# Experts' down projection of a four-layer kernel: weights stationary, output turned back by PE

## The chip, the cores and the metric

One core of one Trainium2 chip runs the whole program in one launch. The metric is the device time of that launch in microseconds (us). The engines are PE (matrix multiply; PEld is its loading of the stationary operand), DVE (vector), ACT (activation), POOL (GpSimd) and SP (which issues DMAs and raises semaphores).

## What is computed

The reference is a chain of four blocks on x of shape (4, 1024, 128), all in float32: `x = x + layernorm(block(layernorm(x)))`, with block = an attention of 16 heads, a latent attention followed by a mixture of experts, a second attention of 16 heads, and a low-rank feed-forward. The change lies in the mixture of experts:

```python
def _experts(x_flat, Wg, Wu, Wd):
    g = silu(einsum('nc,eci->nei', x_flat, Wg))
    u = einsum('nc,eci->nei', x_flat, Wu)
    return einsum('nei,eic->nec', g * u, Wd)
shared = mean(_experts(xf, sWg, sWu, sWd), axis=1)          # one shared expert
probs = softmax(xf @ Wgate + expert_bias)
topk_p, topk_i = top_k(probs, 2); topk_p /= sum(topk_p)
comb = sum(one_hot(topk_i, 8) * topk_p[..., None], axis=1)
routed = einsum('ne,nec->nc', comb, _experts(xf, Wg, Wu, Wd))
return shared + routed                                      # then residual, layernorm, residual
```

There are 8 routed experts and one shared one, of 64 inner columns each, and 128 channels. All of them are computed for every token; the gate weight of a token multiplies the inner columns before the down projection, so that one accumulation over all inner columns gives shared + routed.

## The kernel before, in words

The program is a sequence of phases, each closed by a barrier of all engines (`end_phase`, L109): projection and attention of the first block, the latent attention, `experts()` (L1681 to L1953), projection and attention of the third block (`prepare("a1")` and what follows), and the last block. Semaphores of a phase are made by `sem(name)` (L96), which has SP raise each new one to BASE = 1, one instruction for each (L101).

**Tiling of `experts()`.** The 4096 tokens lie as 32 tiles of 128 tokens on the partitions. The four batch entries b are the bodies of the phase; each has two chunks u of CH = 512 tokens, and a chunk has CT = 4 tiles t. The 9 experts are paired: GP = 5 groups j, four with 128 inner columns (two experts) and one with 64 (the shared one). `run_sequences` (L1721) runs `front(0)`, then a hardware loop over bodies 0 to 2, `body(b, b + 1)`, and then `body(3, None)` apart. Each engine has its own order, written out by hand, and the engines meet only at semaphores.

**PSUM.** It has eight banks of 512 float32 columns. Bank 0 holds turned x or a group's spread gate weights, bank 1 the logits and turned gates, banks 2 and 3 gate projections, 4 and 5 up projections, banks 6 and 7 (`6 + u`) the down projection of chunk u.

**A body on PE** (L1826): for each of the ten (u, j), the gate and up matmuls (L1834, L1836; weights stationary, 512 tokens moving) and the spreading of gate weights (L1841). Then, if a body follows, `logits(b + 1)`: four transposes for each chunk (L446) and eight matmuls with 8 moving columns (L1805). Then the down projection (L1849 to L1855): for each chunk, each of its 4 tiles and each of the 5 groups, a matmul with 128 tokens of `hT` as stationary operand and the 128 channels of `wd` moving. Last `turn_gates(b + 1)` (L1815), which needs the gates from DVE (s_g).

**A body on DVE** (L1922): the ten products silu x up (L1930) and product x gate weight (L1935). Then `front(b + 1)`, the gates of both chunks of the next body (L1878 to L1915, a chain of small instructions that holds one wait on an Exp from ACT). Then for each chunk u: the wait for s_z (chunk turned out by PE), the residual sum that reads bank 6 + u (L1942), and the statistics (L380, L384). Then for each chunk the normalisation (L398) and the residual sum into x (L1950).

**A body on ACT** (L1757): the ten Silu (L1765), with the root mean squares of the next body among them; then `rest_of_front(b + 1)`: two copies of turned x (L1741), two Exp of the gates (L1745), two copies of turned gates (L1748). POOL computes inverse roots (L390, L392, L427, L429).

Each float32 matmul shows in the trace as two records (two passes), a transpose as one. `fill` (L441) issues matmuls whose result nobody reads.

```python
for t in range(CT):
    for j in range(GP):
        rows = P if j < PAIRS else INNER
        i = nc.tensor.matmul(ps[:, 6 + u, t * P:(t + 1) * P],
                             hT[0:rows, u, j, t * P:(t + 1) * P],
                             w_sb["wd"][0:rows, j, :], start=(j == 0), stop=(j == GP - 1))
i.then_inc(s_z, 1)
```

Of the kernel before, what the change touches and what calls it, by code (L numbers as in the profile page):

```python
# [17 lines left out]
P = 128  # L18
# [9 lines left out]
CH = 512  # L28
# [13 lines left out]
BASE = 1  # L42
# [33 lines left out]
def build(nc, ins, consts, out):  # L76
    stack = ExitStack()
    with stack:
# [111 lines left out]
        def work(*shape, dt=F32, parts=P):  # L190

            n = int(np.prod(shape))
            words = n if dt == F32 else (n + 1) // 2
            if hold[0] and area_at[0] < 16384 and area_at[0] + words > 8192:
                area_at[0] = 16384
            a = area[0:parts, area_at[0]:area_at[0] + words]
            area_at[0] += words
            assert area_at[0] <= 24576
            if dt != F32:
                a = a.bitcast(dt)  # L200
            names = "abcde"[:len(shape)]
            if len(shape) > 1:
                a = a.rearrange("p (" + " ".join(names) + ") -> p " + " ".join(names),
                                **{k: v for k, v in zip(names[1:], shape[1:])})
            return a
# [1475 lines left out]
        def experts():  # L1681
# [17 lines left out]
            silu = work(2, CH)  # L1699
            hT = work(2, GP, CH)  # L1700
            ffn = work(2, CT, C)
            s_T = sem(name + "_T")
            s_xT = sem(name + "_xT")
            s_lg = sem(name + "_lg")
# [23 lines left out]
            with nc.Block() as block:  # L1728
                @block.scalar
                def _(act):  # L1730
                    def squares(b, u):
                        rms.squares(act, b, u, tiles_of(x2_res, b, u))

                    def apply(b, u):
                        rms.apply(act, b, u, tiles_of(x2_res, b, u), xr[:, u, :, :], (s_T, 2 * b))

                    def rest_of_front(b):
                        for u in range(2):
                            act.wait_ge(s_T, 2 * b + u + 1 + BASE)
                            act.wait_ge(s_gu, 2 * GP * b + BASE)  # L1740
                            nc.scalar.activation(xrT[:, u, :], ps[:, 0, :], ACT.Copy, scale=w_sb["ln2"][:, 0:1])\  # L1741
                                .then_inc(s_xT, 1)
                        for u in range(2):
                            act.wait_ge(s_g, GATE * (2 * b + u) + 3 + BASE)
                            nc.scalar.activation(prob[:, u, :, :], prob[:, u, :, :], ACT.Exp).then_inc(s_ex, 1)  # L1745
                        for u in range(2):
                            act.wait_ge(s_cT, 2 * b + u + 1 + BASE)
                            nc.scalar.activation(combT[0:SPLIT, u, :], ps[0:SPLIT, 1, :], ACT.Copy)\  # L1748
                                .then_inc(s_cc, 1)

                    def front(b):
                        for step in (squares, apply):
                            for u in range(2):
                                step(b, u)
                        rest_of_front(b)

                    def body(b, following):  # L1757
                        steps = {1: (squares, 0), 2: (squares, 1), GP: (apply, 0), GP + 2: (apply, 1)}
                        for u in range(2):
                            for j in range(GP):  # L1760
                                n = 2 * GP * b + GP * u + j
                                rows = P if j < PAIRS else INNER
                                act.wait_ge(s_gu, n + 1 + BASE)
                                act.wait_ge(s_h, n + 1 + BASE)
                                nc.scalar.activation(silu[0:rows, (GP * u + j) % 2, :],  # L1765
                                                     ps[0:rows, 2 + (GP * u + j) % 2, :], ACT.Silu).then_inc(s_si, 1)
                                if following is not None and GP * u + j in steps:
                                    step, half = steps[GP * u + j]
                                    step(following, half)
                        if following is not None:  # L1770
                            rest_of_front(following)

                    run_sequences(act, body, front)

# [19 lines left out]
                def _(pe):  # L1794
# [31 lines left out]
                    def body(b, following):  # L1826
                        for u in range(2):
                            pe.wait_ge(s_cc, 2 * b + u + 1 + BASE)
                            for j in range(GP):
                                n = 2 * GP * b + GP * u + j  # L1830
                                rows = P if j < PAIRS else INNER
                                r = (GP * u + j) % 2
                                pe.wait_ge(s_h, n + 1 + BASE)
                                nc.tensor.matmul(ps[0:rows, 2 + r, :], w_sb["wg"][:, j * P:j * P + rows],  # L1834
                                                 xrT[:, u, :], start=True, stop=True)
                                nc.tensor.matmul(ps[0:rows, 4 + r, :], w_sb["wu"][:, j * P:j * P + rows],  # L1836
                                                 xrT[:, u, :], start=True, stop=True).then_inc(s_gu, 1)
                                if j < PAIRS:

                                    pe.wait_ge(s_hc, PAIRS * (2 * b + u) + j + BASE)  # L1840
                                    nc.tensor.matmul(ps[:, 0, :], spread[0:SPLIT, j * P:(j + 1) * P],  # L1841
                                                     combT[0:SPLIT, u, :], start=True, stop=True).then_inc(s_cb, 1)
                        if following is not None:
                            logits(following)
                        for u in range(2):
                            pe.wait_ge(s_hc, PAIRS * (2 * b + u + 1) + BASE)
                            pe.wait_ge(s_h, GP * (2 * b + u + 1) + 2 + BASE)
                            pe.wait_ge(s_ff, 2 * b + BASE)
                            for t in range(CT):  # L1849
                                for j in range(GP):  # L1850
                                    rows = P if j < PAIRS else INNER
                                    i = nc.tensor.matmul(ps[:, 6 + u, t * P:(t + 1) * P],  # L1852
                                                         hT[0:rows, u, j, t * P:(t + 1) * P],
                                                         w_sb["wd"][0:rows, j, :], start=(j == 0), stop=(j == GP - 1))
                            i.then_inc(s_z, 1)  # L1855
                        if following is not None:
                            turn_gates(following)
# [417 lines left out]
```

## Time and profile before

| what | value |
|---|---|
| median of 3 runs | 1987.68 us (1985.12 to 1994.09) |
| the profiled execution: its time | 1988.3 us |
| its span in the trace | 1986.6 us |
| mean granted clock of PE | 0.943 of full |
| busy over the span | PE 1712.2 us, PEld 707.0, DVE 1304.7, ACT 1139.2, POOL 668.5 |
| `experts()` in the span | from about 1162.8 to 1354.1 us |

The span is the time between the first and the last instruction of the trace; what the program takes around it is 1.7 us here. Busy time is the time in which an engine had at least one instruction running. "PEclk" in a row is the clock that PE was granted in that stretch, as a share of 2.4 GHz: 1.00 is 2.4 GHz, 0.50 is 1.2 GHz. In a timeline "x80" stands for records merged into one line, and brackets give the idle time of the engine before the line and what ended it.

### The profile page before, as it was taken

To read this page: it belongs to the slowest core of one execution; us is meant where nothing else is said; L and a number is where in the kernel's file an instruction comes from. 1 tells how busy PE (TensorE), PEld (TensorE's weight loads), DVE (VectorE), ACT (ScalarE), POOL (GpSimd) and SP (SyncE) were. 2 spreads that over 40 slices of the span, in tenths; PEclk is the share of its full clock that TensorE was granted. 3 is DMA by queue.
4 is the path that set the end of the run, shared out by engine and by line. 5 is a ranking of instruction groups with operands and counts; after the bars stand their busy time and mean duration, and the time that the engine had idled before them with its cause. 6 is when DMAs were issued, how large, how long until landed. Compare 5 with 4: busy or idle time off the path is not lost. (4 is left out here: it accounts for less than half of the span.)

```text
span 1986.6 us, 41431 instructions
## 1 busy us (share of the span) xinstructions
PE 1712.2 (86%) x12310; PEld 707.0 (36%) x12310; DVE 1304.7 (66%) x2458; ACT 1139.2 (57%) x1786; POOL 668.5 (34%) x1224
## 2 busy tenths in 40 slices
PE   6778787687899999999999888986699898999786
PEld 4312122343334334334333554554333232333132
DVE  6578888583866656656662346665688787888054
ACT  7699999341155545545556344325177676677545
POOL 6365556574212212212222001106122222222364
PEclk9799999798999999999999999898899999999697
DMA  8533235266113213213210410003422221122111
GB/s 242 115 67 63 59 53 141 63 155 143 28 40 65 50 40 65 50 40 65 50 40 23 140 41 1 0 0 99 117 44 47 49 44 42 34 47 68 36 28 43
DMA packets 91800, 125.94 MB, mean 63 GB/s; under 512 B 24501, under 2 KB 63797, under 8 KB 91398
## 3 DMA queue, kind: packets, MB, share of 16 engines
q1 hardware_dynamic: 91622, 123.64, 26.5%
q8 instruction: 103, 1.69, 0.4%
q14 instruction: 75, 0.61, 0.1%
HBM read 75.90 MB, written 47.58 MB: 62 GB/s over the span
## 5 line engine op out<-in xcount | busy, mean ns | idle before, releaser
L1038 ACT ACTIVATE q_buf<-ps 128x1024 f32<-128x1024 f32 (+1 forms) x1152 | 863.4, 822 | 530.9 <-PE ps L922 529.6
L1143 DVE TENSOR_REDUCE o_sb<-ps 128x1 f32<-128x512 f32 (+3 forms) x864 | 718.1, 866 | 272.8 <-PE ps L951 179.8
L1098 POOL TENSOR_SCALAR_AFFINE_SELECT q_buf<-q_buf 128x256 f32<-128x256 f32 x768 | 364.6, 499 | 818.1 <-ACT q_buf L1038 685.1
L971 PE MATMUL ps<-q_buf,v_buf 128*9 128x512 f32 (+7 forms) x4608 | 470.3, 504 | 58.3 <-POOL q_buf L1098 53.9
L922 PE MATMUL ps<-q_buf,k_buf 49*128 49x512 f32 (+3 forms) x1536 | 319.2, 516 | 6.2 <-issue 6.2
L922 PE MATMUL ps<-q_buf 48*128 48x512 bf16 (+7 forms) x1536 | 264.2, 338 | 50.5 <-ACT q_buf L1038 29.2
L1203 DVE TENSOR_SCALAR q_buf<-q_buf 128x1024 f32<-128x1024 f32 x288 | 218.3, 767 | 56.4 <-ACT q_buf L1038 51.4
L922 PEld LDWEIGHTS ps<-q_buf 48*128 48x128 bf16 (+1 forms) x1536 | 76.3, 94 | 309.2 <-ACT q_buf L1038 226.9
L922 PEld LDWEIGHTS ps<-q_buf,k_buf 49*128 49x128 f32 x1536 | 130.5, 187 | 134.7 <-ACT q_buf L1038 66.8
L971 PEld LDWEIGHTS ps<-q_buf,v_buf 128*9 128x9 f32 (+1 forms) x4608 | 92.7, 96 | 239.0 <-issue 119.7
L944 PE MATMUL ps<-k_buf,q_buf 48*128 48x512 bf16 (+3 forms) x768 | 114.2, 330 | 22.3 <-DVE o_sb L1143 15.6
L441 PE MATMUL ps<-w_wg,identity 128*128 128x512 f32 (+1 forms) x214 | 98.5, 582 | 31.4 <-PEq L113 31.4
L944 PE MATMUL ps<-q_buf 48*128 48x512 bf16 (+3 forms) x768 | 115.1, 330 | 2.1 <-DVE o_sb L1143 1.1
L951 PE MATMUL ps<-causal_bf,ident_bf 128*128 128x128 bf16 x1024 | 115.1, 226 | 0.0
L951 PEld LDWEIGHTS ps<-causal_bf,ident_bf 128*128 128x128 bf16 x1024 | 59.0, 99 | 89.3 <-issue 89.3
L944 PEld LDWEIGHTS ps<-k_buf,q_buf 48*128 48x128 bf16 x768 | 38.9, 95 | 139.7 <-DVE o_sb L1143 117.2
L310 DVE BATCH_NORM_STATS2 q_buf<-ps 128x6 f32<-128x128 f32 x96 | 21.3, 285 | 96.7 <-PE ps L2024 71.0
L358 ACT ACTIVATE q_buf<-ps,q_buf 128x128 f32<-128x128 f32 x96 | 36.1, 460 | 61.3 <-POOL q_buf L342 61.3
L446 PE MATMUL ps<-identity,q_buf 128*128 128x128 f32 x160 | 28.0, 302 | 43.7 <-ACT q_buf L358 36.4
L441 PEld LDWEIGHTS ps<-w_wg,identity 128*128 128x128 f32 x214 | 41.4, 219 | 66.2 <-issue 66.2
L1765 ACT ACTIVATE q_buf<-ps 128x512 f32<-128x512 f32 (+1 forms) x40 | 23.8, 596 | 51.7 <-PE ps L1836 51.6
L1852 PE MATMUL ps<-w_wd,q_buf 128*128 128x128 f32 (+1 forms) x320 | 52.9, 313 | 0.0
(178 smaller groups left out, 1561.3 us busy)
## 6 DMA issues: line engine op xcount, KB each, us to landing
q_buf<-qm_d SPq DMA_DIRECT2D x32, 384.0 KB, 6.5
qm_d<-pr_buf SPq DMA_DIRECT2D x80, 128.0 KB, 2.4
o_d<-pr_buf SPq DMA_DIRECT2D x16, 512.0 KB, 2.7
q_buf<-o_d SPq DMA_DIRECT2D x8, 1024.0 KB, 5.1
q_d<-q_buf SPq DMA_DIRECT2D x48, 128.0 KB, 2.1
k_d<-q_buf SPq DMA_DIRECT2D x48, 128.0 KB, 1.9
q_buf<-q_d SPq DMA_DIRECT2D x64, 96.0 KB
q_buf<-k_d SPq DMA_DIRECT2D x64, 96.0 KB
```

Of the source, the lines that this page charges most:

```text
L358: i = nc.scalar.activation(dst[:, t, :], src[:, t, :], ACT.Identity, scale=self.rstd[:, r, t:t + 1], bias=self.minus_m[:, r, t:t + 1])
L441: nc.tensor.matmul(ps[:, bank, 0:columns], identity[:, :], w_sb["wg"][:, 0:columns], start=True, stop=True)
L446: i = nc.tensor.transpose(ps[:, bank, t * P:(t + 1) * P], src[:, t, :], identity[:, :])
L922: mm = nc.tensor.matmul(ps[:, bank + w, off * P:(off + nq) * P], keys(rows, s, p, k), qs[rows, s, p, q0 * P:(q0 + nq) * P], start=True, st ...
L944: mm = nc.tensor.matmul(ps[:, bank[pr], o_ * P:(o_ + nk) * P], (qm if latent else qs)[rows, s, p, q * P:(q + 1) * P], km[rows, s, kk] if l ...
L951: mm = nc.tensor.matmul(ps[:, bank[pr], (o_ + nk - 1) * P:(o_ + nk) * P], ident_bf[:, :], causal_bf[:, :], start=False, stop=True, skip_gr ...
L971: mm = nc.tensor.matmul(ps[VW * j:VW * j + V_ROWS_OUT, o_bank + half % O_BUFS, lo * P:(lo + nq) * P], v, units(i, r, j)[:, 0, off * P:(off ...
L1038: nc.scalar.activation(units(i, g, WIDE * e, WIDE), ps[:, bank:bank + WIDE, :], ACT.Exp, scale=scale).then_inc(s_e, 1)
L1098: nc.gpsimd.affine_select(out=blk, in_=blk, compare_op=ALU.is_ge, fill=0.0, base=0, pattern=[[0, 2], [1, P]], channel_multiplier=-1)\
L1143: nc.vector.tensor_reduce(to, sc, AX_X, ALU.max).then_inc(s_mr, 1)
L1203: nc.vector.tensor_scalar(two, two, float(np.exp(-10.0)), float(np.exp(10.0)), ALU.max, ALU.min).then_inc(s_clip, 1)
L1852: i = nc.tensor.matmul(ps[:, 6 + u, t * P:(t + 1) * P], hT[0:rows, u, j, t * P:(t + 1) * P], w_sb["wd"][0:rows, j, :], start=(j == 0), sto ...
```

## The change

For each chunk, the down projection is now computed with `wd` as stationary operand and the chunk's 512 tokens moving, which leaves the output with channels on the partitions. ACT copies it to SBUF (`downT`), and PE turns it back by four transposes into the same PSUM bank. On PE both chunks' matmuls are issued first, then both chunks' transposes. On ACT the two copies stand behind the Exp of the next body's gates and ahead of the copies of its turned gates; in the last body they stand last. There are two more semaphores (s_dn: matmuls of a chunk done; s_dc: copy of a chunk done); s_z, for which DVE waits, is now raised by the transposes.

```diff
             ffn = work(2, CT, C)
+            downT = work(2, CH)
+            s_dn = sem(name + "_dn")
+            s_dc = sem(name + "_dc")
...
+                    def copy_down(b):
+                        for u in range(2):
+                            act.wait_ge(s_dn, 2 * b + u + 1 + BASE)
+                            act.wait_ge(s_z, 2 * b + BASE)
+                            nc.scalar.activation(downT[:, u, :], ps[:, 6 + u, :], ACT.Copy).then_inc(s_dc, 1)
+
+                    def rest_of_front(b, before=None):
...
                             nc.scalar.activation(prob[:, u, :, :], prob[:, u, :, :], ACT.Exp).then_inc(s_ex, 1)
+                        if before is not None:
+                            copy_down(before)
                         for u in range(2):
                             act.wait_ge(s_cT, 2 * b + u + 1 + BASE)
...
                         if following is not None:
-                            rest_of_front(following)
+                            rest_of_front(following, b)
+                        else:
+                            copy_down(b)
...
                             pe.wait_ge(s_ff, 2 * b + BASE)
+                            for j in range(GP):
+                                rows = P if j < PAIRS else INNER
+                                i = nc.tensor.matmul(ps[:, 6 + u, :], w_sb["wd"][0:rows, j, :], hT[0:rows, u, j, :],
+                                                     start=(j == 0), stop=(j == GP - 1))
+                            i.then_inc(s_dn, 1)
+                        for u in range(2):
+                            pe.wait_ge(s_dc, 2 * b + u + 1 + BASE)
                             for t in range(CT):
-                                for j in range(GP):
-                                    rows = P if j < PAIRS else INNER
-                                    i = nc.tensor.matmul(ps[:, 6 + u, t * P:(t + 1) * P],
-                                                         hT[0:rows, u, j, t * P:(t + 1) * P],
-                                                         w_sb["wd"][0:rows, j, :], start=(j == 0), stop=(j == GP - 1))
+                                i = nc.tensor.transpose(ps[:, 6 + u, t * P:(t + 1) * P],
+                                                        downT[:, u, t * P:(t + 1) * P], identity[:, :])
                             i.then_inc(s_z, 1)
```

## Rows read from the trace of the kernel before

**Rows 1.** Groups of instructions, 1162 to 1354 us: busy, mean ns, idle before.
```profile
L1852 PE MATMUL ps<-w_wd,q_buf 128*128 128x128 f32 (+1 forms) x320 | 52.9, 313 | 0.0
...
L446 PE MATMUL ps<-identity,q_buf 128*128 128x128 f32 x32 | 5.1, 281 | 3.7 <-ACT q_buf L1741 3.7
```
**Rows 2.** Timeline of PE in body 2 and into body 3: start, length in us.
```profile
1298.95 12.08 PE L1852 MATMUL ps<-w_wd,q_buf 128*128 128x128 f32 x80
1310.95 0.41 PE L1815 MATMUL ps<-ident_bf,q_buf 128*72 128x128 bf16 x4
...
1319.32 0.39 PE L1841 MATMUL ps<-q_buf 72*128 72x512 bf16 x1 [3.04 <-DVE q_buf L1935]
```
**Rows 3.** Timeline of DVE in body 2 and the start of body 3.
```profile
1309.84 0.19 DVE L1915 TENSOR_TENSOR q_buf<-q_buf 128x32 bf16<-128x32 f32 x1
1310.12 0.69 DVE L1942 TENSOR_TENSOR q_buf<-ps,v_buf 128x512 f32<-128x512 f32 x1
...
1312.20 0.69 DVE L1942 TENSOR_TENSOR q_buf<-ps,v_buf 128x512 f32<-128x512 f32 x1
...
1317.86 0.68 DVE L1930 TENSOR_TENSOR q_buf<-ps,q_buf 128x512 f32<-128x512 f32 x1
```
**Rows 4.** Timeline of ACT in body 2 and the start of body 3.
```profile
1295.80 0.69 ACT L1741 ACTIVATE q_buf<-ps,w_ln 128x512 f32<-128x512 f32 x1
...
1305.21 0.23 ACT L1745 ACTIVATE q_buf<-q_buf 128x32 f32<-128x32 f32 x1 [5.18 <-DVE q_buf L1882]
1311.40 0.59 ACT L1748 ACTIVATE q_buf<-ps 72x512 bf16<-72x512 f32 x1 [5.97 <-PE ps L1815]
...
1314.40 0.60 ACT L1765 ACTIVATE q_buf<-ps 128x512 f32<-128x512 f32 x1
```
**Rows 5.** Timeline of PE: a chunk of x turned; 512-column matmuls.
```profile
1295.02 0.66 PE L446 MATMUL ps<-identity,q_buf 128*128 128x128 f32 x4
1296.63 0.63 PE L446 MATMUL ps<-identity,q_buf 128*128 128x128 f32 x4 [0.96 <-ACT q_buf L1741]
...
1332.11 1.02 PE L1834 MATMUL ps<-q_buf,w_wg 128*128 128x512 f32 x2
1332.97 1.02 PE L1836 MATMUL ps<-q_buf,w_wu 128*128 128x512 f32 x2
```
**Rows 6.** Timeline of PE and DVE in the last body, to the next phase.
```profile
1336.38 12.10 PE L1852 MATMUL ps<-w_wd,q_buf 128*128 128x128 f32 x80
1342.50 0.69 DVE L1942 TENSOR_TENSOR q_buf<-ps,v_buf 128x512 f32<-128x512 f32 x1 [4.71 <-PE ps L1852]
...
1348.51 0.69 DVE L1942 TENSOR_TENSOR q_buf<-ps,v_buf 128x512 f32<-128x512 f32 x1 [3.93 <-PE ps L1852]
...
1353.42 0.69 DVE L1950 TENSOR_TENSOR x_res<-x_res,q_buf 128x512 f32<-128x512 f32 x1
```
**Rows 7.** Timeline of PE and DVE in body 1.
```profile
1252.42 16.65 PE L1852 MATMUL ps<-w_wd,q_buf 128*128 128x128 f32 x80
1263.59 0.69 DVE L1942 TENSOR_TENSOR q_buf<-ps,v_buf 128x512 f32<-128x512 f32 x1
1269.22 0.69 DVE L1942 TENSOR_TENSOR q_buf<-ps,v_buf 128x512 f32<-128x512 f32 x1 [3.55 <-PE ps L1852]
```
**Rows 8.** Stretches: length; PE, PEld, DVE, ACT, POOL busy; PEclk; DMA share; GB/s.
```profile
1253.40:1263.40 10.00, 10.00 (x38) 8.21 (x37) 8.54 (x35) 0.33 (x2) 0.00 (x0) 0.50 0.00 0
...
1171.40:1178.20 6.80, 6.80 (x13) 3.35 (x13) 4.78 (x21) 0.23 (x1) 0.00 (x0) 0.50 0.00 0
...
1277.40:1280.60 3.20, 3.20 (x5) 1.16 (x4) 0.54 (x2) 0.77 (x3) 0.47 (x1) 0.50 0.00 0
```
**Rows 9.** The same view: product loops of bodies 2 and 3, as DVE passes them.
```profile
1274.96:1296.42 21.46, 18.56 (x43) 6.95 (x43) 12.25 (x19) 10.29 (x34) 2.53 (x4) 0.92 0.00 0
1317.94:1337.79 19.85, 17.79 (x49) 7.16 (x49) 12.25 (x18) 4.76 (x8) 0.00 (x0) 1.00 0.00 1
```
**Rows 10.** SP's raising of semaphores at the start of the phase.
```profile
L101 SPq EVENT_SEMAPHORE  x26: 17/17/17, 1162.8 to 1164.7; - x26
```

More of the change, by code:

```diff
@@ L1735, in apply @@
                         rms.apply(act, b, u, tiles_of(x2_res, b, u), xr[:, u, :, :], (s_T, 2 * b))
-                    def rest_of_front(b):
+                    def copy_down(b):
[4 more added lines that the diff above has]
+                    def rest_of_front(b, before=None):
                         for u in range(2):
```

## The prediction

> **What bounds the kernel now.** I read the groups of instructions of the phase first, then the timelines of its bodies, then the clock in short stretches. The groups say what is for sale: the down projection is 320 records and 52.9 us of busy PE [rows 1], in a phase of about 191 us in a run of 1988.3. PE is the busiest engine, which tempts one to book all that it saves. The timelines say otherwise. In body 2 the down projection runs from 1298.95 to 1311.03 [rows 2], but in those 12 us DVE works without a pause at the next body's gates, to 1310.03 [rows 3], then at once at the chunk sum L1942 (1310.12), the second L1942 (1312.20), norms and residuals, and at 1317.86 at the next body's first product [rows 3]. No idle time stands before any of these rows. The first Silu of body 3 was done at 1315.0 [rows 4], 2.9 us before DVE came for it. So from the gates to the next body's products **DVE sets the time** and PE is cover. Body 0 has the same pattern.
>
> There are two exceptions. In the **last body** no gates are left: DVE waits 4.71 and then 3.93 us for the down projection [rows 6], and the phase ends 5.60 us after the second L1942 starts (1353.42 + 0.69 = 1354.11). In **body 1** the clock fell to 0.50, 1.2 GHz, at 1253.4 and came back at 1263.4 [rows 8], after the transposes and 8-column matmuls of `logits`; the same 80 records took 16.65 us in place of 12.08, and DVE waited 3.55 us for chunk 1 [rows 7].
>
> **The change, part by part.**
>
> Matmuls. Before, a chunk is 4 tiles x 5 groups x 2 passes = 40 passes; 80 take 12.08 us [rows 2], so 0.151 us each and 6.04 us a chunk. After, it is 5 groups x 2 = 10 passes of 512 columns. The gate matmul of this size starts 0.86 us before the next pair [rows 5], so 0.43 us a pass and 4.3 us a chunk; the end of the last pass comes some 0.16 us behind its slot (1.02 against 0.86). Four transposes of a chunk, first start to end, take 0.66 us [rows 5]; as records merged they are 5.1 us for 32 [rows 1], or 0.16 each. I take 0.66 where they are exposed, and about 0.45 as throughput (4 x 0.11, the lengthening of 0.66 over one record of 0.28, shared by three).
>
> PE time. 6.04 - 4.3 - 0.45 = 1.3 us a chunk, 10.4 us over eight.
>
> Copies. 8 on ACT, 128x512 from PSUM: between 0.59 (the 72-row copy) and 0.69 (the scaled one) [rows 4]; I take 0.60. In a loop body they stand behind the second Exp, which is due at 1305.21 whatever PE does, since DVE's gates set it, and ACT idles 5.97 us after it [rows 4]. They add 1.2 us to that gap. Behind them in ACT's queue wait the copies of the turned gates, on which PE's next body waits. From PE to ACT a handover takes 0.12 us, from ACT to PE 0.14 (1295.68 to 1295.80, 1296.49 to 1296.63) [rows 4, 5].
>
> A loop body at full clock, on body 2's times: matmuls from 1298.95, chunk 0 done at about 1303.4, chunk 1 at 1307.7. ACT copies chunk 0 at 1305.5 and chunk 1 at 1307.8 to 1308.4. PE turns chunk 0 from 1307.6 to 1308.2 and chunk 1 from 1308.5 to 1309.2. DVE needs them at 1310.12 and 1312.20, so the slack is 1.9 and 3.0 us, and PE then idles 0.9 us for the gates of 1310.03. `turn_gates` starts at 1310.1 in place of 1310.95, and so do the next gate and up matmuls and the first Silu; that goes into the 2.9 us that Silu already waits for DVE. **Gain 0**, for bodies 0 and 2. If the cover were gone (gates shorter by 2 us), the turning would be late by what exceeds the slack.
>
> Last body: matmuls from 1336.38, both chunks done at 1336.38 + 8.6 + 0.16 = 1345.1. Here the new order costs something: chunk 0's turning stands behind chunk 1's matmuls. Its transposes run from 1344.95 to 1345.6, so DVE starts chunk 0 at 1345.65 in place of 1342.50. Chunk 1 is copied by 1345.9 and turned by 1346.7, but DVE needs 2.08 us for chunk 0 (1310.12 to 1312.20) [rows 3] and comes at 1347.73, in place of 1348.51 [rows 6]. **Gain 0.8 us**. Bounds: 1.3 if DVE could start chunk 0 with the end of the matmuls, and a loss of 0.4 if each chunk's copy and turning stood bare behind the matmuls with two handovers more (1345.1 + 2 x 1.5 + 0.7 for the sum against 1348.51).
>
> Body 1, if the clock falls there again. The 20 passes need 8.6 us, and each us at half clock adds 0.5. How long the clock stays low is seen three times: 10.0 us under the 128-column matmuls, 6.8 under 512-column fills, 3.2 under 512-column gate and up matmuls [rows 8]. The new passes are like the latter two. At 6.8: 1252.42 + 8.6 + 3.4 + 0.16 = 1264.6, chunk 0 turned at 1265.2, DVE at chunk 1 by 1267.3 in place of 1269.22, gain 1.9. At 3.2 the turning ends before the gates (1263.5), and chunk 1 comes at 1263.59 + 2.08 = 1265.67, gain 3.55. At 10.0 the gain is 0.3. I take the middle of the two like cases, **2.7 us**; the ends are 0 (or nothing to save, where no fall meets a body) and 3.55 for each body that one meets.
>
> Of the clock the trace shows that it fell after transposes and 8-column matmuls although PE was busy. The Trainium skill ("TensorE: Matmul & The Clock Gate", Part 4: PE-mode transpose) says that work in transpose mode does not count as PE-busy in the same way. By that rule the 32 new transposes would help the clock to fall, against the change; the sum by it is the third rival's. No row here has transposes without small matmuls beside them, so it is open.
>
> Semaphores: SP raises 26 between 1162.8 and 1164.7 [rows 10], 0.075 us each; two more make 0.15 us beside the first squares and fills. The order of the activation tables stays, as a Copy stands already after Exp and after Silu. SBUF space, DMAs and POOL's and SP's queues are otherwise untouched. Nothing.
>
> **Sum** on the profiled execution: 1988.3 - 0.8 - 2.7 = **1984.8 us**. That execution is 0.6 above the median of 1987.68 and well inside 1985.12 to 1994.09; 0.5% (10 us) is about what a measurement of this kernel can tell from no change. I do not shift the sum by 0.6, as the fall's place differs between runs.
>
> **The rivals.**
>
> *A. The tail only.* The clock falls as before, and the 512-column passes do not bring it back sooner, or no fall meets a down projection. For it: one of three loop bodies met it. Against: the two shorter stretches of 512-column work [rows 8]. Time 1988.3 - 0.8 = 1987.5 to 1987.2.
>
> *B. PE's time counts in full.* If PE were the bound in every body, the eight chunks would give 10.4 us: 1977.9. The busy share speaks for it, DVE's timeline without gaps against it [rows 3]; it would need an L1930 that waits for Silu at the start of a body. The Trainium skill ("Perfetto Trace Analysis", Identifying the Most-Contended Engine) advises to optimise the most occupied engine first, for PE by its weight loads. Here that would make PE, whose loads fall from 320 to 112, the place to save; DVE's rows say that it is not.
>
> *C. Slower: the clock falls in most bodies.* PE now idles 0.9 us before the gates' turning and has transposes beside it, and after two groups of the next body it idles again until DVE comes, which was 3.04 us [rows 2] and would be 3.9. In body 2 such a spot cost a fall at 1277.4 [rows 8] and a product loop of 21.46 us against 19.85 [rows 9], 1.6 us. A fall at the down projection that lasted 10 us would put chunk 1 at 1268.9 in place of 1265.67, 3.2 us. Both together are 4.8 a body; the trace of before holds 3.55 + 1.6 = 5.15 of such loss. With two bodies: 9.6 - 5.15 - 0.8 = +3.65, 1992.0; with three: 14.4 - 5.95 = +8.45, 1996.8. It decides from the second body on. Against it: denser matmuls in the 8.6 us before.
>
> **How the numbers follow.** Forecast 0.50, A 0.30, B 0.07, C 0.13. The range takes in the forecast's ends (1988.3 - 1.3 - 3.55 = 1983.5, and one such fall more avoided: 1980), A, and C to its lower case: 1980 to 1992. It leaves out B, C with three bodies, and a few runs' scatter. Faster by over 0.5% (below 1977.7) is B with a little luck: 0.05. Slower by over 0.5% (above 1997.6) is C's end and past it: 0.03. Within: 0.92.
>
> **What would show it.** The 512-column passes of the down projection at 0.43 us, 8.6 us a body at full clock; L1942 of chunk 0 in loop bodies right behind the gates, with no wait for PE; in the last body L1942 about 9.3 and 11.35 us after the matmuls' start (before: 6.1 and 12.1); `turn_gates` waiting for DVE. Wrong would be a wait before L1942 in a loop body at full clock, a wait for Silu before a body's first product, or a low clock in two or more loop bodies.

## The result, and the profile after

The changed kernel is slower: median 1997.01 us (1987.09 to 2006.05, 20 runs) against 1987.75 us (1983.00 to 2000.84, 20 runs) for the kernel before, ratio 1.0035 with a 95% interval of 1.0019 to 1.0051, or some 7 us by the ratio. The forecast was 1984.8 us with a range to 1992. The profiled execution after took 2006.05 us, the longest of its 20. 13 us of its surplus over the profile before lie in the latent attention, which the change does not touch and which took 639 to 653 us in all profiles of this study. So the comparison is made in the experts phase, by profiles of several kernels.

Engines over the span, of the page after:

```profile
PE 1725.5 (86%) x12102; PEld 689.6 (34%) x12102; DVE 1303.4 (65%) x2458; ACT 1143.8 (57%) x1794; POOL 667.6 (33%) x1224
```

Groups of instructions of the changed kernel in its experts phase (records; busy us, mean ns; idle before):

```profile
L1864 PE MATMUL ps<-q_buf,w_wd 128*128 128x512 f32 (+1 forms) x80 | 40.3, 648 | 0.0
...
L1870 PE MATMUL ps<-identity,q_buf 128*128 128x128 f32 x32 | 5.3, 287 | 0.4
...
L1744 ACT ACTIVATE q_buf<-ps 128x512 f32<-128x512 f32 x8 | 4.8, 597 | 18.1 <-PE ps L1864 18.1
```

The change does what it says: 80 records in place of 320, 32 transposes, 8 copies of 0.60 us. PE is busy 45.6 us with the down projection and its turning in place of 52.9 [rows 1].

Timeline of the changed kernel, PE (with one row of DVE), end of body 0 and start of body 1 (start, length in us; idle before):

```profile
1224.12 9.42 PE L1864 MATMUL ps<-q_buf,w_wd 128*128 128x512 f32 x20
1233.47 1.41 PE L1870 MATMUL ps<-identity,q_buf 128*128 128x128 f32 x8
1235.25 0.41 PE L1828 MATMUL ps<-ident_bf,q_buf 128*72 128x128 bf16 x4 [0.37 <-DVE q_buf L1932]
...
1244.82 0.61 PE L1854 MATMUL ps<-q_buf 72*128 72x512 bf16 x1 [3.98 <-DVE q_buf L1952]
1245.22 1.92 PE L1847 MATMUL ps<-q_buf,w_wg 128*128 128x512 f32 x2
1246.93 1.91 PE L1849 MATMUL ps<-q_buf,w_wu 128*128 128x512 f32 x2
...
1249.51 0.69 DVE L1947 TENSOR_TENSOR q_buf<-ps,q_buf 128x512 f32<-128x512 f32 x1 [3.33 <-ACT q_buf L1776]
```

The turning of the gates (L1828) now waits for DVE, as the forecast said. So do the two groups behind it, done sooner, and PE stands idle 3.98 us where it stood 3.04 [rows 2]. In that idle the clock falls, the gate and up matmuls take 1.9 us each (two passes) in place of 1.0 [rows 5], and DVE waits 3.33 us for Silu. (The 3.04 us are of body 3; ahead of body 1, which is shown here, the kernel before had 3.13.)

Stretches of the changed kernel (length; PE, PEld, DVE, ACT, POOL busy; PEclk): the phase, the product loops of bodies 1, 2 and 3, and the fall in the first of them:

```profile
1175.97:1371.56 195.59, 165.23 (x462) 71.22 (x462) 115.17 (x336) 68.42 (x175) 22.48 (x34) 0.91 0.00 0
1243.25:1265.67 22.42, 19.43 (x43) 7.38 (x43) 12.32 (x19) 8.88 (x25) 2.46 (x4) 0.85 0.00 0
1243.30:1250.00 6.70, 5.18 (x8) 2.29 (x9) 3.10 (x6) 1.12 (x6) 1.14 (x2) 0.50 0.00 0
1287.08:1309.77 22.69, 19.70 (x43) 7.43 (x43) 12.32 (x19) 8.88 (x25) 2.47 (x4) 0.85 0.00 0
1333.54:1355.04 21.50, 19.48 (x43) 7.10 (x44) 12.32 (x19) 4.76 (x8) 0.00 (x0) 0.92 0.00 0
```

and of the kernel before, the phase and the product loops of bodies 1, 2 and 3:

```profile
1162.21:1354.43 192.22, 166.86 (x670) 94.46 (x670) 115.40 (x336) 63.77 (x167) 21.90 (x34) 0.94 0.00 0
1229.58:1249.90 20.32, 17.03 (x43) 6.38 (x43) 12.34 (x19) 9.12 (x27) 2.53 (x4) 1.00 0.00 0
1274.88:1296.43 21.55, 18.56 (x43) 6.95 (x43) 12.33 (x19) 10.38 (x34) 2.53 (x4) 0.92 0.00 0
1317.86:1337.79 19.93, 17.79 (x49) 7.16 (x49) 12.33 (x19) 4.76 (x8) 0.00 (x0) 1.00 0.00 1
```

A product loop is the stretch from a body's first L1930 (L1947 after) to the end of its last one. All three that follow a body have a fall of the clock, and take 22.42, 22.69 and 21.50 us; before they took 20.32, 21.55 with the only fall, and 19.93 (the stretches of rows 9 start 0.08 us late). A loop of body 3 is 0.4 us shorter than the others even without a fall, so loops are compared body by body. The phase is 3.4 us longer.

Last body, timeline of the changed kernel, PE, its weight loads and DVE:

```profile
1353.63 9.44 PE L1864 MATMUL ps<-q_buf,w_wd 128*128 128x512 f32 x20
1357.26 0.29 PEld L1864 LDWEIGHTS ps<-q_buf,w_wd 64*128 64x128 f32 x2 [0.76 <-issue]
1358.31 0.30 PEld L1864 LDWEIGHTS ps<-q_buf,w_wd 128*128 128x128 f32 x2 [0.76 <-issue]
1363.69 0.69 DVE L1959 TENSOR_TENSOR q_buf<-ps,v_buf 128x512 f32<-128x512 f32 x1 [8.65 <-PE ps L1870]
1365.68 0.66 DVE L1959 TENSOR_TENSOR q_buf<-ps,v_buf 128x512 f32<-128x512 f32 x1
1370.55 0.69 DVE L1967 TENSOR_TENSOR x_res<-x_res,q_buf 128x512 f32<-128x512 f32 x1
```

The second sum starts 12.05 us after the matmuls' start, against 12.13 before [rows 6]: nearly nothing is gained there.

### The profile page after: what moved, and what is told of

The parts are those of the page before. It is cut to its first block and busy times, and to the rows that moved or that the text cites. A ratio compares the mean times of both kernels' runs of the same rounds, so it can differ in the third digit from the quotient of the medians.

```text
span 2004.1 us, 41037 instructions
## 1 busy us (share of the span) xinstructions
PE 1725.5 (86%) x12102; PEld 689.6 (34%) x12102; DVE 1303.4 (65%) x2458; ACT 1143.8 (57%) x1794; POOL 667.6 (33%) x1224
## 5 line engine op out<-in xcount | busy, mean ns | idle before, releaser
L1143 DVE TENSOR_REDUCE o_sb<-ps 128x1 f32<-128x512 f32 (+3 forms) x864 | 718.1, 865 | 290.0 <-PE ps L951 192.2
L922 PE MATMUL ps<-q_buf,k_buf 49*128 49x512 f32 (+3 forms) x1536 | 323.6, 522 | 6.7 <-issue 6.7
L441 PE MATMUL ps<-w_wg,identity 128*128 128x512 f32 (+1 forms) x214 | 107.8, 629 | 31.2 <-PEq L113 31.2
L944 PE MATMUL ps<-k_buf,q_buf 48*128 48x512 bf16 (+3 forms) x768 | 119.1, 343 | 16.0 <-DVE o_sb L1143 8.8
L1947 DVE TENSOR_TENSOR q_buf<-ps,q_buf 128x512 f32<-128x512 f32 (+1 forms) x40 | 27.5, 688 | 38.4 <-ACT q_buf L1776 38.4
```

The lines of the kernel that those rows point to most:

```text
L441: nc.tensor.matmul(ps[:, bank, 0:columns], identity[:, :], w_sb["wg"][:, 0:columns], start=True, stop=True)
L922: mm = nc.tensor.matmul(ps[:, bank + w, off * P:(off + nq) * P], keys(rows, s, p, k), qs[rows, s, p, q0 * P:(q0 + nq) * P], start=True, st ...
L944: mm = nc.tensor.matmul(ps[:, bank[pr], o_ * P:(o_ + nk) * P], (qm if latent else qs)[rows, s, p, q * P:(q + 1) * P], km[rows, s, kk] if l ...
L1143: nc.vector.tensor_reduce(to, sc, AX_X, ALU.max).then_inc(s_mr, 1)
L1947: nc.vector.tensor_tensor(hT[0:rows, u, j, :], ps[0:rows, 4 + r, :], silu[0:rows, r, :], ALU.mult).then_inc(s_h, 1)
```

## The experiments

One experts phase holds three product loops, and falls come and go between runs, so most kernels run the phase six times over, and what is computed is then not the reference's, since x has the experts' output added six times:

```diff
-experts()
-end_phase()
+for turn in range(6):
+    experts(turn)
+    end_phase()
```

In the table, the first column of falls counts the stretches of PEclk 0.50 that begin in the product loops of bodies 1 to 3 or in the 3 us ahead, of 18; the second counts, of 18 too, the tails of bodies 0 to 2 in which one begins earlier than that. A fall is such a stretch. The tail is the rest of a body, from the end of its product loop to its last L1950; it is averaged over bodies 0 to 2, with the falls in it, and given by itself for body 3. All is read from one profile each; the time is the median of the kernel's 6 runs. The first three rows and the one with 4 fills were timed on one chip, the others on three more, on which the kernel before took 1988.8 to 1993.3 us; so a difference between rows of different chips can be off by some 7 us (an estimate from that spread of 0.2%).

| six phases of | a phase, us | product loop, us | falls | tail, us | falls | last tail, us | time, us |
|---|---|---|---|---|---|---|---|
| kernel before | 194.6 | 20.75 | 8 | 22.68 | 10 | 16.31 | 2967.7 |
| changed kernel | 196.9 | 21.92 | 17 | 22.39 | 10 | 16.21 | 2983.5 |
| before, 3 tiles | 189.1 | 20.78 | 7 | 21.76 | 18 | 13.32 | 2934.7 |
| 3 tiles + transposes | 189.1 | 20.47 | 4 | 21.85 | 15 | 14.30 | 2944.3 |
| 3 tiles + matmuls | 190.7 | 20.65 | 6 | 22.14 | 16 | 14.41 | 2945.7 |
| changed, turned by matmuls | 198.3 | 21.69 | 17 | 22.92 | 15 | 16.71 | 2985.3 |
| changed, 1 fill in the idle | 197.8 | 21.62 | 17 | 22.89 | 11 | 16.21 | 2975.2 |
| changed, 2 fills | 195.0 | 20.46 | 4 | 22.58 | 10 | 16.22 | 2961.8 |
| changed, 4 fills | 192.6 | 20.19 | 0 | 21.80 | 6 | 16.20 | 2958.8 |
| changed, 4 fills, not in body 0 | 191.7 | 20.19 | 0 | 22.22 | 10 | 16.21 | 2940.9 |
| before, 4 fills, not in body 0 | 196.4 | 21.09 | 0 | 22.91 | 12 | 16.32 | 2981.8 |

**Is it this phase?** The kernel before, six phases:

> The kernel before with the experts phase run six times over in place of once (its output is therefore not the reference's): 24 bodies in one profile, as a scale for the next run. Theory I (idle and clock): the added time of the change comes from this phase, because PE, done sooner with the down projection, idles longer ahead of each body's second group and the clock falls in the product loop more often; here about one product loop in three shows a fall, and a phase takes 191 to 193 us. Theory II (elsewhere): the added time lies in phases that the change does not touch, by placement or chance; then this kernel and the next one agree within 2 us over the six phases.

The changed kernel, six phases:

> The changed kernel with its experts phase run six times over. Theory I: at least two of three product loops that follow a body show a fall of the clock to 0.5, each costing 1.6 to 2.4 us; a phase takes 194 to 197 us, and the whole is 15 to 30 us slower than the kernel before with six phases. Theory II: the same as that kernel within 2 us. My own forecast of 3.5 us gained a phase would show as 21 us faster.

Measured: 2967.67 us (2957.47 to 2990.21) and 2983.49 us (2973.28 to 2993.54), 16 us apart, 2.6 a phase; by the profiles 2.3. Theory I had said 15 to 30 us and two of three loops with a fall; there were 17 of 18, against 8 of 18. For the kernel before I had expected 191 to 193 us a phase and a fall in one loop of three; it took 194.6 us, with 8 of 18. The differences add up: three product loops give 3 x (21.92 - 20.75) = +3.5, three tails 3 x (22.39 - 22.68) = -0.9, the last tail -0.1, in sum +2.5. Theory II, that nothing arises here, falls, and so does my forecast of a gain.

Both kinds of body are seen without a fall too: there both kernels' tails take 21.5 us, and their loops of bodies 1 and 2 take 20.31 (of the changed kernel it is one loop; the fills below give more). So at full clock the change moves nothing in a loop body.

**What makes the clock fall: three tiles of four.** The down projection of the kernel before leaves out the last 128 tokens of a chunk:

```diff
-for t in range(CT):
+for t in range(CT - 1):
```

> Six phases of the kernel before, but the down projection leaves out the fourth tile of each chunk: 60 passes of 128 columns, about 9.1 us in place of 12.08, with no transposes and no copies. It tells what of the change makes the clock fall. Theory Ia (idle): PE being done 3 us sooner is enough; PE waits for the gates before their turning, the idle ahead of the second group is near 4 us, falls in product loops are as frequent as in the changed kernel, and a phase takes 193 to 196 us. Theory Ib (transposes do not keep the clock up): without transposes the falls are as rare as in the kernel before, and a phase takes 188 to 192 us, the last body alone giving some 3 us.

Neither theory fitted: 7 falls of 18 (Ia had asked for many), though PE is done 3 us sooner. The timeline of PE around body 1 shows what came in between:

```profile
1224.54 0.41 PE L1815 MATMUL ps<-ident_bf,q_buf 128*72 128x128 bf16 x4 [2.06 <-DVE q_buf L1915]
1225.64 0.60 PE L1815 MATMUL ps<-ident_bf,q_buf 128*72 128x128 bf16 x4 [0.68 <-ACT q_buf L1748]
1226.22 2.07 PE L1834 MATMUL ps<-q_buf,w_wg 128*128 128x512 f32 x2
...
1234.12 0.39 PE L1841 MATMUL ps<-q_buf 72*128 72x512 bf16 x1 [2.55 <-DVE q_buf L1935]
```

and the stretch in which the clock was low:

```profile
1225.80:1229.10 3.30, 3.30 (x8) 1.53 (x7) 2.96 (x16) 1.88 (x2) 1.47 (x3) 0.50 0.00 0
```

Here the idle is split: 2.06 us ahead of the gates' turning, and the rest ahead of the second group. The clock falls once in the first idle, and while it is low the two groups run slowly, for which DVE does not care; that shortens the second idle to 2.55 us. 18 of 18 tails had a fall, most of them hidden: the tails took 21.76 us on average. A fall costs what DVE waits for behind it.

Taken body by body, this run comes near to theory Ia after all. In 9 of the 18 bodies the low stretch lay as above, ending less than 8 us ahead of the next product loop; none of these 9 loops had a fall. Of the other 9 loops, 7 had one. With the two runs that follow, which also have three tiles, it is 0 of 19 loops behind such a late low stretch, and 17 of 35 without one. A low stretch just ahead of the loop thus goes with no fall in it.

**Transposes or ordinary matmuls.** To the three tiles were added, a chunk, either four transposes

```diff
+for t in range(CT):
+    i = nc.tensor.transpose(ps[:, 6 + u, 3 * P:4 * P], hT[:, u, 0, t * P:(t + 1) * P], identity[:, :])
```

> Six phases of the kernel before with three of four tiles in the down projection and four transposes a chunk behind them (of hidden columns, so that their result is not the reference's). PE's course in time is near that of the changed kernel, about 10.3 us from first matmul to last transpose against 10.8, without ACT's copies. Theory Ib (transposes decide): falls in 15 or more of 18 product loops of bodies 1 to 3, 21.6 us or more on average. Theory Ic (it is when PE is busy and idle relative to the clock's own course, whatever it does): the same count as in the next run.

or two float32 matmuls:

```diff
+for j in range(2):
+    i = nc.tensor.matmul(ps[:, 6 + u, 3 * P:4 * P], hT[:, u, j, 3 * P:4 * P],
+                         w_sb["wd"][:, j, :], start=(j == 0), stop=(j == 1))
```

> The same, but with two ordinary float32 matmuls a chunk (four passes of 128 columns, 0.6 us) in place of the four transposes, so that the fourth tile holds two of its five groups. The same course in time within 0.2 us a chunk. Theory Ib: 9 or fewer of 18 product loops show a fall, 20.9 us or less on average. Theory Ic: the same count as in the run before, high or low.

Measured: 4 and 6 falls in product loops, 15 and 16 in tails, 2944.28 and 2945.70 us. Transposes make no more falls than matmuls of about the same length (Ib had asked for 15). From the other side, the changed kernel with its transposes done as matmuls against the identity:

```diff
-i = nc.tensor.transpose(ps[:, 6 + u, t * P:(t + 1) * P], downT[:, u, t * P:(t + 1) * P], identity[:, :])
+i = nc.tensor.matmul(ps[:, 6 + u, t * P:(t + 1) * P], downT[:, u, t * P:(t + 1) * P], identity[:, :],
+                     start=True, stop=True)
```

> Six phases of the changed kernel with the eight transposes of a body done as ordinary float32 matmuls against the identity (two passes each of 128 columns, 2.4 us in place of 1.4). Theory Ib: the falls in product loops drop from 17 of 18 to 9 or fewer, a phase below 195 us. Theory Ic: the turning ends 1 us later and the gates' turning some 0.6 us later, so the count can change either way, but falls do not vanish; a phase of 194 to 198 us.

17 falls again, 198.3 us a phase, 2985.26 us, with idles of 3.1 to 4.1 us. **Theory Ib is out**: the transposes are not what lets the clock fall here.

**Filling the idle.** Ahead of the second group's spreading (u = 0, j = 1) PE waits until the turned gates are copied, and issues n matmuls that nobody reads (`fill(1, n)`; here with n = 4, then 1 and 2):

```diff
+if u == 0 and j == 1:
+    pe.wait_ge(s_cc, 2 * b + 2 + BASE)
+    fill(1, 4)
 pe.wait_ge(s_hc, PAIRS * (2 * b + u) + j + BASE)
```

> Six phases of the changed kernel with four float32 matmuls of 512 columns (3.4 us of PE) that nobody reads, issued in each body ahead of the second group's spreading, where PE otherwise idles for about 4 us. Theory Ia: no fall in a product loop any more, 5 to 7 us a phase regained against the changed kernel, a phase of 188 to 191 us. Theory Ib: falls stay, since the transposes before still count for nothing, and the time stays within 1 us a phase. Theory II: no difference.

> Six phases of the changed kernel with one float32 matmul of 512 columns (0.86 us) that nobody reads ahead of the second group's spreading, so that PE's idle there is near 3.1 us, as in the kernel before, while the transposes stay. Theory Ia (the length of the idle decides): falls in about half of the product loops, as in the kernel before (8 of 18) and not as in the changed one (17 of 18); those loops take 20.7 to 21.2 us on average against 21.92. Theory Ib (the transposes decide): 15 or more of 18 still show a fall, 21.7 us or more.

> Six phases of the changed kernel with two idle-filling matmuls (1.7 us; idle left near 2 us) ahead of the second group. With one, 17 of 18 product loops still showed a fall; with four, none. If the idle's length widens the stretch in which a fall can be met, the count is between, 3 to 12 of 18, and a phase takes 193 to 196 us.

With four, no fall in 18 product loops, 4.3 us a phase below the changed kernel and 24.7 us in the whole (2958.78 us). I had expected 5 to 7 us and 188 to 191 us a phase; body 0 has next to no idle at that spot (0.35 us), and there the fills cost 2.9 us. PE's timeline with four:

```profile
1239.62 3.60 PE L441 MATMUL ps<-w_wg,identity 128*128 128x512 f32 x8
1243.65 0.39 PE L1856 MATMUL ps<-q_buf 72*128 72x512 bf16 x1 [0.44 <-DVE q_buf L1954]
1243.88 1.02 PE L1847 MATMUL ps<-q_buf,w_wg 128*128 128x512 f32 x2
```

and with one:

```profile
1231.94 1.02 PE L441 MATMUL ps<-w_wg,identity 128*128 128x512 f32 x2
1235.64 0.39 PE L1856 MATMUL ps<-q_buf 72*128 72x512 bf16 x1 [2.68 <-DVE q_buf L1954]
1235.87 1.77 PE L1847 MATMUL ps<-q_buf,w_wg 128*128 128x512 f32 x2
```

With one fill, idle is 2.5 to 3.2 us, and yet 17 of 18 loops had a fall: against theory Ia as I had put it. The kernel before says the same. Its idles are of two lengths: behind 1.9 to 2.1 us 6 of 10 loops had a fall, behind 2.8 to 3.2 us only 2 of 8, where one fill leaves as long an idle and nearly every loop had one. With two, 1.6 to 2.3 us are left in 17 of the 18, and 4 loops had a fall. So without the idle there is no fall, but its length alone does not give the count, and what makes it 17 with the new order and 8 with the old one stays open. What differs with the length is where falls begin: in the kernel before 0.8 to 1.4 us after the second group's first matmul; in the changed kernel, with idles of 3.3 to 4.0 us, from 1.8 us before it to 1.4 us after; with one fill, 16 of 17 after it. My reading, argued and not shown, is that a longer idle leaves more places at which the clock can fall, and that which of them a body meets depends on where the last fall ended, since a body's length changes with the falls in it. For it speaks that the fourth and fifth phases of the changed kernel repeat one another, loop for loop, within 0.1 us, and that a late low stretch kept 19 of 19 loops with three tiles free of a fall.

**Fills only where there is an idle.** PE's loop has body 0 written out ahead of it, without fills:

```diff
-if u == 0 and j == 1:
+if u == 0 and j == 1 and not (isinstance(b, int) and b == 0):
...
-run_sequences(pe, body, front)
+front(0)
+body(0, 1)
+with pe.Fori(1, BATCH - 1) as b:
+    body(b, b + 1)
+body(BATCH - 1, None)
```

> Six phases of the changed kernel with four matmuls in the idle of bodies 1 to 3 only (PE's loop has body 0 written out ahead of it, where that spot has no idle and the four cost 2.9 us). Theory Ia: no falls in product loops of bodies 1 to 3, the loop of body 0 back at 20.3 us, a phase of 189 to 190.5 us and a whole of 2940 to 2950 us, some 35 us below the changed kernel and 20 below the kernel before with six phases. Theory II: no difference.

> The same four matmuls in bodies 1 to 3 of the kernel before, six phases. What is left between this and the changed kernel with them is what the new down projection is worth once the clock is held: my forecast's mechanism gives the new one the advantage, through shorter loss where a fall meets the down projection (before: 10 of 18 loop bodies, 1.15 us each on average) and 0.1 us in the last body; 1 to 4 us a phase. Were the four matmuls late, they would push the second group by up to 0.5 us a body here, since this kernel's idle is 3.1 us, shorter than the 3.4 us of the matmuls. A phase of 191 to 194 us.

2940.90 us for the changed kernel, 42.6 below it unfilled and 26.8 below the kernel before with six phases, as expected (2940 to 2950; by the ratios to the kernel before on each chip it is 40 and 28 us); the phase, at 191.7, missed its bracket through 10 falls in tails. The kernel before became slower, 2981.76: its idle of 1.9 to 3.2 us does not hold fills of 3.4, so that there were no falls in product loops, but the second group came late and loops took 21.09 us; the phase, at 196.4, missed its bracket of 191 to 194. The same fills gain in one and lose in the other. Shorter fills, which would fit the idle of the kernel before, were not run there. By its loops without a fall (20.19 us on average over the three bodies, against 20.75) they could give it up to 1.7 us a phase, an estimate, so that part of what the changed kernel gains by fills is not due to the change.

One phase, as in the change:

> The changed kernel with one experts phase, as in the change, and the four matmuls in bodies 1 to 3. Theory Ia: the phase takes 188 to 189.5 us (195.6 in the changed kernel, 192.2 in the kernel before), and the whole is 2 to 5 us faster than the kernel before, ratio 0.997 to 1.000. Theory II: 1.002 to 1.005, as the changed kernel.

Phase 189.07 us, no fall in a product loop; whole 1990.65 us against 1989.68, ratio 1.0002 (0.9977 to 1.0026). The loss of the change can no longer be told from nothing; the 2 to 5 us of gain that I had expected did not come, and a version that beats the kernel before is not shown, though its phase is 3 us shorter in the one profile.

**Where the rest arises.** The changed kernel and the kernel before once more:

> The changed kernel once more, for a second profile. If the course of the clock is set by the kernel's own course (theory Ic, and Ib), the experts phase repeats its 195.6 us within 1 us, with a fall in each of the product loops of bodies 1 to 3, while the phases before and after it differ from the first profile by several us (the latent attention took 652.6 us there against 639 to 647 in five others). Theory II (the added time lies elsewhere) would need the latent attention near 652 us again. Ratio 1.002 to 1.005.

> The kernel before once more, for another profile of it: an experts phase of 190 to 193 us, with a fall in one of three product loops or none, the phases ahead of it within 5 us of the first profile. Its ratio to the kernel before is 1 within its interval, which shows how much of the changed kernel's 1.004 such a comparison can invent.

1.0040 (1.0019 to 1.0062) with a phase of 196.01 us and three falls; 1.0003 (0.9986 to 1.0019) with 192.44 us and one. The sums repeat, but the loops do not: the changed kernel's took 22.42, 22.69 and 21.50 us in the first profile and 22.78, 21.91 and 21.98 in the second, and the kernel before had its one fall in body 2 first and in body 3 then. And both kernels cut off behind the experts phase, with x stored as it stands there and the last two blocks left out:

```diff
-prepare("a1")
...
-finish_and_ffn()
+s_last = count("last")
+with nc.Block() as block:
+    @block.sync
+    def _(sp):
+        for c in range(CHUNKS):
+            sp.dma_start(out.rearrange("b (t p) c -> p (b t) c", p=P)[:, c * CT:(c + 1) * CT, :],
+                         tiles(x_res, c)).then_inc(s_last, 16)
+        sp.wait_ge(s_last, 16 * CHUNKS)
```

> The kernel before, cut off after the experts phase: what is stored is x as it stands there, and the third and fourth block are left out. The time is near 1365 us. With the next run it tells whether all of the 7 us of the change arises by the end of the experts phase. First phase by the profiles so far: 190.9 to 192.2 us.

> The changed kernel, cut off in the same way. If the experts phase alone is the cause, this is 4 to 5 us slower than the run before (195.6 to 196.0 us in three profiles against 190.9 and 192.2), and what the whole kernels differ by beyond that, 3 us, is chance or arises later, where the next phases meet the clock at another point. If something ahead of the phase is slowed as well, the difference is 7 us or more.

1367.60 us (1364.81 to 1372.09) and 1373.92 (1369.68 to 1384.64): 6.3 us apart, five runs each, with ranges that overlap. That lies between the 4 to 5 us set for the phase alone and the 7 set for a cause ahead of it as well, and decides neither. The phases took 190.51 and 194.28 us, the latter below the 195.6 to 196.0 seen till then. Over all profiles, the first experts phase of the kernel before took 192.2, 192.4, 190.5 and 190.9 us, that of the changed one 195.6, 196.0, 194.3 and 195.6: **3.9 us** apart (the last of each from the six-phase profiles). Product loops with a fall were 3 of 9 against 9 of 9 in the single-phase ones.

The other 3 us or so of the ratio I can't place. All that stands ahead of the phase took 1165.1 us on average (8 profiles with the old down projection or parts of it) and 1167.4 (10 with the new one), all that stands behind it 629.9 (7) and 632.6 (9), with standard errors of 1.2 to 1.7. Neither difference is clear of chance. Code ahead of the phase is the same; behind it, the next phases meet the clock at another point of its course. That is argued, not shown.

## Why the prediction was wrong

**What failed is a cost that the sum held at nothing.** "Gain 0, for bodies 0 and 2": PE's earlier end in loop bodies was booked as going into the time that Silu waits for DVE. It does, but it also lengthens PE's idle ahead of the second group, from 1.9 to 3.2 us to 3.3 to 4.0. The clock falls in that idle or just behind it, and a product loop with a fall takes 1.2 to 2.5 us more than one of the same body without. In place of nothing the product loops lost 3 x 1.17 = 3.5 us a phase over six phases, more in a single phase, where 9 of 9 loops had a fall against 3 of 9. Shown are the place, the price, and that no loop has a fall once matmuls fill the idle. Not shown is that the added length makes the falls more frequent: one fill took it away again, and 17 of 18 loops still had one.

This is the first half of **rival C**, which I had at 0.13, with its place (ahead of the second group), its cause (PE idle until DVE comes) and its price (1.6 us, against 1.3 to 2.5 in the changed kernel over a loop of the same body without a fall). That the price came near is in part luck: 21.46 against 19.85 set a loop of body 2 beside one of body 3, and against a loop of body 1 or 2 without a fall the one fall had cost 21.55 - 20.32 = 1.2 us. What I got wrong was its chance, and that I tied it to long falls at the down projection, which did not come. The trace of before had the sign: one of three idles of 1.9 to 3.1 us had a fall behind it, and the change lengthens idles of that kind, to the 3.9 us that I had worked out myself. It was not a sign that longer idles are worse, as the fall stood behind the shortest of the three (kernel before, timeline of PE, body 2):

```profile
1276.45 0.39 PE L1841 MATMUL ps<-q_buf 72*128 72x512 bf16 x1 [1.88 <-DVE q_buf L1935]
```

**The matmuls**: 0.43 us a pass was right, but a chunk takes 4.7 us and not 4.3. Passes of groups with 128 rows start 0.43 us apart; at a change between a 128-row group and the 64-row one, either way, two passes start 0.52 to 0.53 us after the one before, some 0.1 us late each. (The weight loads there have 0.76 us of idle before them, in place of 0.24, but most of that is hidden behind the pass that runs.) Seven such steps make the 0.7 us by which both chunks take 9.42 us in place of the 8.76 that I had. My 0.11 us for a further transpose did not follow from its own division either, 0.38 by three is 0.13; that takes some 0.5 us off the 10.4 of rival B and changes nothing else.

**Last body**: forecast 0.8 us, measured 0.1 (16.31 to 16.21 us). Nearly all of the missing gain is those 0.7 us of matmuls: the first sum started 10.06 us after the matmuls' start, forecast 9.27.

**Loop bodies at full clock**: gain 0 as to the tail, right: 21.5 us in both. The transposes of both chunks ended 0.4 us ahead of the gates' turning, not 0.9, for the same reason.

**A fall at the down projection**: forecast 2.7 us for one. Measured over six phases: 10 tails of 18 met one in either kernel; the low stretches were 3.4 to 13.7 us long before (mean 6.8) and 3.4 or 6.8 after (mean 5.1), so the denser passes do go with shorter ones. Over all profiles none of 68 low stretches in the tails with the new order was longer than 6.83 us, and 16 of 76 with the old one or parts of it were. But for the same length the new order costs more (medians 22.18 against 22.04 us at 3.4, 23.85 against 23.59 at 6.8), perhaps because chunk 0's turning stands behind chunk 1's matmuls. What is left is 0.3 us a body, 0.9 a phase, or 0.5 for each fall met. The term was mis-sized by a factor of three for the phase and of five for one fall, and its price taken from a 10 us case that was among the rarer ones.

**Rivals A and B**: A had no cost in it, and fell. B (PE's time in full) was rightly small: PE is busy 7.3 us less with this work, and the program is slower. The advice that I set beside B, from the Trainium skill ("Perfetto Trace Analysis", Identifying the Most-Contended Engine), judges PE by its share of peak arithmetic and by its weight loads, not by its busy matmuls, and I misapplied it: the loads were busy 707.0 us before and DVE 1304.7, so that by the loads it did not point to PE.

**The rule on transposes.** The Trainium skill ("TensorE: Matmul & The Clock Gate", Part 4: PE-mode transpose) says that a transpose does not count as PE-busy in the same way. No effect of it is seen here: 4 against 6 falls with transposes or matmuls behind three tiles, 17 and 17 in the changed kernel. The same page of the Trainium skill ("Why this matters for your kernels") warns of idle gaps between bursts of matmuls; the fills agree in the main (17 falls with no fill, none with four), while 17 falls with one fill show that the length of the idle alone does not tell. I had weighed the rule that does not matter here and passed by the one that does.

## What to carry to other kernels

Work saved on an engine that is not the bound is not free: if the engine is PE, ask what its longer idle does to the clock, and book the next burst at both clocks. Before such a change, list the idles of PE that it lengthens and see whether any of that kind already has a fall behind it; its length alone does not tell. Filling an idle with matmuls pays only where the fill fits the idle: the same four gained 5 us a phase by the profiles and 7 by the times in one version (2983.5 to 2940.9 us over six) and lost 2 in the other.

## What the runs showed that I had not expected

- One low stretch seems to prevent another: with three tiles in the down projection, 0 of 19 loops had a fall behind a low stretch that ended less than 8 us ahead, against 17 of 35 others. Most of these low stretches were free, since DVE did not wait for the groups that they slowed.
- The length of the phase repeats between independent runs, 195.6 and 196.0 us for the changed kernel and 192.2 and 192.4 for the kernel before, although the falls sit in other bodies and cost each loop another amount. A third pair was 1.3 and 1.7 us shorter (194.3 and 190.5).
- Changing a float32 stationary operand from 128 rows to 64 and back costs some 0.2 us each way between 512-column passes, although the weight load itself comes 0.5 us late.
